# Attention's softmax sums on GpSimd: order of adds and joins, a third buffer of parts, later totals

## The reference

```python
c_q  = h_t @ W_DQ + b_DQ;   c_kv = h_t @ W_DKV + b_DKV        # 32 wide
q = concat(c_q @ W_UQ + b_UQ, c_q @ W_QR + b_QR)              # 8 heads of 128 + 32
k = concat(c_kv @ W_UK + b_UK, h_t @ W_KR + b_KR)
v = c_kv @ W_UV + b_UV
attn = softmax(q @ k.T / sqrt(160), axis=-1)
x = x + (attn @ v) @ W_O + b_O
```

## Time and profile before

| | |
|---|---|
| median of 3 runs | 766.88 us (766.19 to 766.91) |
| profiled execution | 765.69 us |
| its span, first to last instruction | 763.5 us |
| mean granted clock of TensorE | 0.984 |
| busy: PE, DVE, ACT, POOL | 94%, 76%, 60%, 72% |
| attention's loop of blocks | about 38 to 519 us of the span |

### The profile page before, as it was taken

The page is one execution under the profiler, slowest core; times in us unless marked ns, Lnnn a source line. Parts: engine busy times, 40 slices in busy tenths (PEclk is TensorE's granted clock), DMA queues, the critical chain, the costliest instruction groups (busy, mean ns, idle before and its releaser), DMA issues.

```text
span 763.5 us, 12866 instructions
## 1 busy us (share of the span) xinstructions
PE 718.2 (94%) x4432; PEld 480.1 (63%) x4432; DVE 583.6 (76%) x1211; ACT 461.3 (60%) x1069; POOL 550.8 (72%) x451
## 2 busy tenths in 40 slices
PE   7979999989989999989999998859989999999997
PEld 6655555655656566555566555427656679788885
DVE  7878788877877888878888887454788835868885
ACT  4257667756665776755775665634667860455553
POOL 6447888878778888878888887941679872346674
PEclk9999999999999999999999999979999999999999
DMA  6213647547546646645645745714000000022430
GB/s 151 80 36 60 127 86 137 112 84 138 112 84 117 132 84 125 126 84 107 136 91 111 139 85 111 139 28 115 1 0 2 1 1 1 1 65 80 134 111 28
DMA packets 41672, 64.17 MB, mean 84 GB/s; under 512 B 16380, under 2 KB 25613, under 8 KB 37640
## 3 DMA queue, kind: packets, MB, share of 16 engines
q0 software_dynamic: 12896, 48.76, 32.6%
q1 hardware_dynamic: 27432, 14.48, 7.2%
q10 hardware_dynamic: 1280, 0.12, 0.1%
HBM read 13.35 MB, written 1.10 MB: 19 GB/s over the span
## 4 chain that ended last, share of the span: by engine, by line
POOL 32%; DMA 28%; PE 24%; issue 8%; DVE 6%; ACT 1%; POOLq 0%; ACTq 0%; DVEq 0%
DMA part<-prob 27%; POOL part L929 10%; POOL w_v L951 8%; POOL hid_lo L1028 4%; POOL w_v L955 4%; PE ps L1898 4%; PE ps L1538 2%; POOL nrm L1008 2%; PE ps L1494 2%; PE ps L1938 2%; DVE mx L1082 2%; PE ps L1940 2%; PE ps L1939 2%; PE ps L1480 1%; POOL hid L1008 1%
## 5 line engine op out<-in xcount | busy, mean ns | idle before, releaser
L1082 DVE TENSOR_REDUCE mx<-ps 128x1 f32<-128x512 f32 x492 | 303.6, 681 | 77.2 <-PE ps L1480 77.1
L643 ACT ACTIVATE prob<-ps 128x512 f32<-128x512 f32 x512 | 263.2, 615 | 123.2 <-PE ps L1494 105.2
L1494 PE MATMUL ps<-q_cols,key 128*128 128x512 f32 x512 | 213.1, 420 | 12.8 <-ACT prob L643 12.8
L1480 PE MATMUL ps<-key,q_rows 128*128 128x512 f32 x512 | 206.3, 408 | 2.1 <-DVE key L1068 1.6
L929 POOL TENSOR_TENSOR part<-prob 128x512 f32<-128x512 f32 x128 | 184.1, 1496 | 1.5 <-ACT prob L643 1.0
L1494 PEld LDWEIGHTS ps<-q_cols,key 128*128 128x128 f32 x512 | 96.9, 190 | 80.0 <-issue 34.1
L1538 PE MATMUL ps<-prob,val 128*32 128x512 f32 x1024 | 124.6, 604 | 0.0
L1480 PEld LDWEIGHTS ps<-key,q_rows 128*128 128x128 f32 x512 | 97.0, 190 | 29.3 <-DVE mx L1082 9.9
L951 POOL TENSOR_TENSOR w_v<-part,pair 128x1024 f32<-128x1024 f32 x31 | 74.1, 2391 | 50.4 <-DMA part<-prob 50.4
L943 POOL TENSOR_TENSOR pair<-prob 128x512 f32<-128x512 f32 x62 | 87.7, 1567 | 5.1 <-ACT prob L643 5.1
L1028 POOL TENSOR_TENSOR hid_lo<-hid,hid_hi 128x512 fp32r<-128x512 f32 x44 | 61.5, 1407 | 38.7 <-ACT hid_hi L809 38.6
(11 more groups left out here) (284 smaller groups left out, 1129.7 us busy)
## 6 DMA issues: line engine op xcount, KB each, us to landing
part<-prob POOLq DMA_DIRECT2D x31, 1024.0 KB, 7.4
w_v<-part POOLq DMA_DIRECT2D x31, 512.0 KB, 4.9
g_all<-g_rows SPq DMA_DIRECT2D x9, 256.0 KB, 3.2
den<-den_sb SPq DMA_DIRECT2D x124, 0.5 KB, 1.8
g_all<-g_rows SPq DMA_DIRECT2D x6, 224.0 KB, 3.0
X<-in_L_attn_h_t_dram SPq DMA_DIRECT2D x4, 256.0 KB, 4.0
out_dram<-X SPq DMA_DIRECT2D x4, 256.0 KB, 2.6
g_all<-g_rows SPq DMA_DIRECT2D x6, 128.0 KB, 3.0
```

The source lines that it names most:

```text
L643: act.activation(prob[:, g % RING, :], ps[:, g % 3, :], ACT.Exp, scale=SCALE).then_inc(s_exp, 1)
L1082: dve.tensor_reduce(mx[:, n % 2, c % TPB, at:at + 1], ps[:, BANK["rows", 2 * lin + j], :], AX.X, ALU.max).then_inc(s_mrd, 1)
L1480: pe.matmul(ps[:, BANK["rows", 2 * lin + j], :], q_rows[:, k, i * P:(i + 1) * P], key[:, h % KBUF, c0:c0 + BLK], start=True, stop=True).th ...
L1494: pe.matmul(ps[:, g % 3, :], key[:, n // NB % KBUF, t * P:(t + 1) * P], q_cols[:, n % NB, :], start=True, stop=True).then_inc(s_sc, 1)
```

## The change

- GpSimd's list in block n becomes: parts 0, 1, 2, 3, `add_pairs(n-1)`, `late_sums(n)`, pair 0, pair 1, `join_parts(n-1)`. `add_pairs` writes in place into the parts, and the join goes from parts 1, 3 into parts 0, 2.
- `part` becomes a list of three buffers; the third lies in `w_v`, where `fin` was.
- totals(n-2) moves from slot 1 to the end of slot 6; its copy by ScalarE goes to tile 14; output moves from slot 6 (n-2) to slot 1 (n-3), and VectorE's denominators and accumulate from slot 6 to slot 2. Their items in the rotation of banks move along.
- `row_pairs` and `key_parts`: block 0 makes one chunk per slot and one key; the two further chunks and the key are made in blocks 1 and 2.
- Blocks 28 and 29 are not joined: TensorE sums four parts. In block 30 VectorE adds tiles 8-11 and 12-15 to the parts, and GpSimd only makes the parts.

```diff
--- before.py
+++ after.py
@@ -195,20 +195,22 @@
 
         def row_pairs(n, slot):
 
-            first = CPB * n + slot + LEAD + (min(slot // 2, AHEAD) if n == 0 else AHEAD)
-            count = 2 if n == 0 and slot in range(1, 2 * AHEAD, 2) else 1
+            first = CPB * n + slot + LEAD + min(max(n - 1, 0), AHEAD) + (1 if 1 <= n <= AHEAD and slot > 2 else 0)
+            count = 2 if 1 <= n <= AHEAD and slot == 2 else 1
             return [lin for lin in range(first, first + count) if lin < NCHUNK]
 
         def key_parts(n, slot):
 
-            if n == 0 and slot in (0, 4):
-                return [NB + slot // 4]
+            if n == 2 and slot == 4:
+                return [n + KLEAD]
+            if n <= 2:
+                return [n + NB] if slot == 0 else []
             return [n + KLEAD] if slot == 0 and n + KLEAD < H * NB else []
         U = 7
         A_BANK = (4, 2)
         KB_AT = H * C1
         prob = sb("prob", [P, RING, BLK])
-        part = sb("part", [P, 2, NG, BLK])
+        part_sb = sb("part", [P, 2, NG, BLK])
         pair = sb("pair", [P, 2, BLK])
         den_sb = sb("den_sb", [P, BLK])
         den = sb("den", [P, 2, TPB])
@@ -225,11 +227,11 @@
 
         def begun(n):
 
-            return 4 if n == 0 else 5 * n + 4
+            return 4 if n == 0 else 5 * n + 3
 
         def paired(n):
 
-            return 5 * n + 7
+            return 5 * n + 9
         s_join = sem("s_join")
         s_usb, s_ops, s_rden, s_acc = sem("s_usb"), sem("s_ops"), sem("s_rden"), sem("s_acc")
         s_ones, s_densb, s_dend = sem("s_ones"), sem("s_densb"), sem("s_dend")
@@ -238,7 +240,7 @@
 
 
 
-        SUMS_AT, OUT_AT = 1, 6
+        JOINED = NBLK - 4
 
         BANK, BEFORE, holds = {}, {}, {}
 
@@ -258,9 +260,13 @@
                     todo.append(("queries", n + 2))
                 if slot == 5 and n == 0:
                     todo += [("folded", 0), ("folded", 1)]
-                if slot == SUMS_AT and 2 <= n < NBLK - 1:
+                if slot == 1 and 3 <= n < NBLK - 1:
+                    todo.append(("out", n - 3))
+                if slot == 1 and n == NBLK - 2:
                     todo.append(("sums", n - 2))
-                if slot == OUT_AT and 2 <= n < NBLK - 1:
+                if slot == 6 and 2 <= n < NBLK - 2:
+                    todo.append(("sums", n - 2))
+                if slot == 6 and n == NBLK - 2:
                     todo.append(("out", n - 2))
             for item in todo:
                 place_item(item, 3 + turn % 4)
@@ -389,7 +395,7 @@
         AT_TW = D + E
         s_sc1, s_d1, s_e1, s_gt_ps, s_gt, s_gtl, s_z0 = (sem(n) for n in ("s_sc1", "s_d1", "s_e1", "s_gt_ps", "s_gt", "s_gtl", "s_z0"))
 
-        fin = w_v[:, :, :].rearrange("p (x h) d -> p x (h d)", x=TPB)[:, 0:2, :]
+        part = [part_sb[:, 0], part_sb[:, 1], w_v[:, :, :].rearrange("p (x h) d -> p x (h d)", x=NG)]
         with nc.sbuf_tensor("pT", [P, HP, S], F32) as pT:
             pass
         act_g = sb("act_g", [P, 2, BLK])
@@ -505,9 +511,12 @@
                     with nc.allow_non_contiguous_dma("128 x 4 words into one row"):
                         sp.dma_start(q_cols[SH:SH + 1, k, :].bitcast(F32).rearrange("a (p i) -> a p i", i=TPB),
                                      nmx[:, n % 2, :].bitcast(F32)).then_inc(s_shift, 16)
-                    if n >= 2:
+                    if 3 <= n < NBLK - 1:
+                        denominators(n - 3)
+                    if n == NBLK - 2:
                         denominators(n - 2)
 
+                denominators(NBLK - 3)
                 denominators(NBLK - 2)
 
 
@@ -637,7 +646,10 @@
                         act.wait_ge(s_sum, begun(n - 1))
                     elif g >= RING and t == 2 * NG:
                         act.wait_ge(s_pv, NW * n)
-                        act.wait_ge(s_late, 16 * n)
+                        if n < NBLK - 1:
+                            act.wait_ge(s_late, 16 * n)
+                        else:
+                            act.wait_ge(s_pair, 2 * n - 1)
                     elif g >= RING and t == 3 * NG:
                         act.wait_ge(s_pair, 2 * n)
                     act.activation(prob[:, g % RING, :], ps[:, g % 3, :], ACT.Exp, scale=SCALE).then_inc(s_exp, 1)
@@ -671,7 +683,7 @@
                     for t in range(NT):
                         if t == 4 and n >= 1:
                             sums(n - 1)
-                        if t == 2 * SUMS_AT + 2 and n >= 2:
+                        if t == (14 if n < NBLK - 2 else 4) and n >= 2:
                             sums_out(n - 2)
                         if t == 10 and n == NBLK - 1:
                             sums_out(n - 1)
@@ -923,16 +935,16 @@
 
                 def begin_sum(n, g):
 
-                    if n >= 2 and g == 0:
-                        pool.wait_ge(s_join, 16 * (n - 1))
+                    if n >= 3 and g == 0:
+                        pool.wait_ge(s_ones, n - 2)
                     ready(n, 2 * g + 1)
-                    pool.tensor_tensor(part[:, n % 2, g, :], tiles(n, 2 * g, 1)[:, 0, :], tiles(n, 2 * g + 1, 1)[:, 0, :], ALU.add).then_inc(s_sum, 1)
+                    pool.tensor_tensor(part[n % 3][:, g, :], tiles(n, 2 * g, 1)[:, 0, :], tiles(n, 2 * g + 1, 1)[:, 0, :], ALU.add).then_inc(s_sum, 1)
 
                 def late_sums(n):
 
                     ready(n, 3 * NG - 1)
                     pool.wait_ge(s_sum, begun(n))
-                    pool.dma_start(part[:, n % 2, :, :], tiles(n, 2 * NG, NG), accum_op=ALU.add).then_inc(s_late, 16)
+                    pool.dma_start(part[n % 3], tiles(n, 2 * NG, NG), accum_op=ALU.add).then_inc(s_late, 16)
 
                 def add_pair(n, j):
 
@@ -946,29 +958,32 @@
 
                     pool.wait_ge(s_late, 16 * (n + 1))
                     pool.wait_ge(s_pair, 2 * (n + 1))
+                    p = part[n % 3][:, bass.ds(0, 2, step=2), :]
+                    pool.tensor_tensor(p, p, pair[:, :, :], ALU.add).then_inc(s_sum, 1)
+
+                def join_parts(n):
+
+                    pool.wait_ge(s_sum, paired(n))
                     if n >= 1:
-                        pool.wait_ge(s_ones, n)
-                    pool.tensor_tensor(fin, part[:, n % 2, bass.ds(0, 2, step=2), :], pair[:, :, :], ALU.add).then_inc(s_sum, 1)
-
-                def join_parts(n):
-                    pool.wait_ge(s_sum, paired(n))
-                    pool.dma_start(fin, part[:, n % 2, bass.ds(1, 2, step=2), :], accum_op=ALU.add).then_inc(s_join, 16)
+                        pool.wait_ge(s_join, 16 * n)
+                    pool.dma_start(part[n % 3][:, bass.ds(0, 2, step=2), :], part[n % 3][:, bass.ds(1, 2, step=2), :],
+                                   accum_op=ALU.add).then_inc(s_join, 16)
 
                 for n in range(NBLK):
                     begin_sum(n, 0)
                     if n < 2:
                         columns(n + 2)
                     begin_sum(n, 1)
-                    if n >= 1:
+                    begin_sum(n, 2)
+                    begin_sum(n, 3)
+                    if 1 <= n < NBLK - 1:
                         add_pairs(n - 1)
-                    begin_sum(n, 2)
-                    if n >= 1:
-                        join_parts(n - 1)
-                    begin_sum(n, 3)
-                    if n < NBLK - 1:
+                    if n < NBLK - 2:
                         late_sums(n)
                         add_pair(n, 0)
                         add_pair(n, 1)
+                    if 1 <= n <= JOINED:
+                        join_parts(n - 1)
                     if n == NBLK - 2:
                         ln0_pool(pool, 0)
                 pool.memset(anchors2[:, :], 0.0).then_inc(s_aside, 1)
@@ -1088,6 +1103,16 @@
                     if n >= 2:
                         dve.wait_ge(s_shift, 16 * (n - 1))
                     dve.tensor_reduce(nmx[:, n % 2, :], mx[:, n % 2, :, :], AX.X, ALU.max, negate=True).then_inc(s_sel, 1)
+
+                def late_sums(n, j):
+
+                    at = (NT * n + NG * (2 + j)) % RING
+                    if j == 0:
+                        dve.wait_ge(s_sum, begun(n))
+                    else:
+                        dve.wait_ge(s_pair, 2 * n + j)
+                    dve.wait_ge(s_exp, NT * n + NG * (3 + j))
+                    dve.tensor_tensor(part[n % 3], part[n % 3], prob[:, at:at + NG, :], ALU.add).then_inc(s_pair, 1)
 
                 def key_biases(m, bank):
                     heads = slice(4 * m, 4 * (m + 1))
@@ -1175,13 +1200,18 @@
                             chunk_max(lin)
                         if slot == 2 and n == 0:
                             values()
-                        if slot == 5 - AHEAD and n < NBLK - 1:
+                        if CPB * (n + 2) - 1 in lins:
                             minus_max(n + 1)
-                        if slot == OUT_AT and 2 <= n < NBLK - 1:
+                        if slot == 2 and 3 <= n < NBLK - 1:
+                            denominators(n - 3)
```

(35 more changed lines are left out.)

1 line of the change is left out of this document (removed).

## The result

The changed kernel takes 786.95 us (786.48 to 787.2, 4 runs) beside 766.54 for the kernel before in the same set; the ratio is 1.0271 [1.0252, 1.0289]. The forecast of 772.7 had the sign right and under a third of the size: +5.8 against +20.4. The profiled run took 787.2, its span 785.5. Against 763.5 before, the landmarks of ScalarE's timeline say where the 22.0 are.

The account below looks back on a forecast made before the run. It took TensorE to set the steady blocks, with the late DMA costing 11.95 in all. Terms +15.1, +1.3, -7.3 and -3.3 sum to +5.8, so 766.88 + 5.8 = 772.7, range 768 to 777.

Parts of the forecast that it names:

- The pause and the bank order: Slot 3 of each steady block: TensorE's second row matmul waits for VectorE's accumulate, 1.78 lost, net +1.05 per block.
- The step that failed: Totals' den transfers, from slot 7 to slot 2: 7 us available where 3.8 are needed, so no wait.
- +15.1: The 24 blocks with keys: 15.03 each, 360.7 in all instead of 345.62.
- +1.3: The three blocks without keys: 14.55 each, 43.65 in all instead of 42.35.
- The old long blocks: Four of 27 blocks lasting 15.4 to 17.4, tile 8's exponential waiting for the late DMA; said to disappear.
- The join: Last on GpSimd's queue each block; said to have more than a block until its totals in slot 6.
- The end: Last blocks: TensorE's 9.61 wait and half clock go, -12.4, against +5.1 of new work; net -7.3 (-9 to -4).
- the bound of 4.7: VectorE's late sums in block 30: 4.7 each instead of 2.2 would add 2.5; the forecast took 0.
- The start: Blocks 0 to 2: block 0 about 5.1 shorter, blocks 1 and 2 take back 1.8; net -3.3 (-5 to 0).
- The clock rival: Steady blocks: the new pause drops TensorE's granted clock in 11 of 28 blocks, 16 more, 788.7; chance 0.22.
- the stated whole: Whole program: 766 to 790, leaving out the two faster cases and the worst of the clock.
- The pause does not form: Slot 3: VectorE reads the out bank before TensorE wants it, 27 x 1.78 = 48 less, 725; chance 0.10.

Follow-up runs that it names:

- Run 4: Changed kernel with the late DMA of tiles 8 to 11 adding only 64 of 512 columns (an eighth of its bytes); 778.49 us.
- run 6: Changed kernel with totals of n-2 in slot 1 of every block; 860.4 us with accumulation in slot 1, 909.08 us with it in slot 2.
- run 9: Block 30's tiles 8 to 15 given back to GpSimd, without VectorE's late sums: 787.94 us on the changed kernel, 748.45 with accumulation in slot 1, totals in slot 4.
- run 1: Changed kernel with only the totals two slots earlier, in slot 4; accumulation stays in slot 2; 787.21 us.
- Run 5: Changed kernel with the late DMA cut to an eighth of its bytes and accumulation in slot 1; totals stay in slot 6; 735.84 us.
- Run 3: Changed kernel with both accumulation in slot 1 and totals in slot 4; 744.75 us.
- run 2: Changed kernel with only VectorE's denominators and accumulation moved from slot 2 to slot 1; 783.33 us.

## Why the prediction was wrong in size

In the profiled executions +5.8 became +22.0. Of the 16.2 between them 8.7 are the five long blocks, 3.1 the even blocks, 2.2 the end, 0.3 the start, and 1.7 the clock's fall in the FFN, which has nothing to do with the change.

- **The pause and the bank order held.** Place, releaser and number (28) are as worked out. It is 1.53 of idle; from start to start it costs 1.70, and 0.10 more at the start behind it: 1.80, where 1.78 was worked out. The even block is 15.15 against 15.03, and 14.60 against 14.55, as the bank waits that went away were some 0.63 and not 0.73: 24 x 0.12 = 2.9 too little, and 0.15 in the other three.
- **The step that failed** is "Totals and the den transfers that SP issues start at slot 7 and have 7 us until slot 2, where 3.8 are needed." The 3.8 were read where these transfers lay beside the end of the late DMA alone. The change moves them towards its start, and the join by DMA behind them. Each lands in 4.0 at the median and 5.0 at most, the four take 3.7 to 5.7 to issue, and the last lands 5.5 to 8.6 behind the first issue: there were 7.8 until the reciprocal (7.3 without keys), a little more than the 7, and five times that was not enough. The step was put at nothing in the sum. In the 24 blocks four long ones hold 2.29 + 2.27 + 0.71 + 0.51 = 5.8, which with the 2.9 makes 8.7 of the 8.8 between +15.1 and +23.9. The fifth holds 2.9 of the 3.1 between +1.3 and +4.4. Run 4 takes the large transfer away and gets 8.5 back. The old long blocks, where ScalarE waited for the late DMA, did disappear as forecast; new ones of another cause came. I had counted what each queue issues, and not what is in flight when it does.
- **The join** was said to have "more than a block until its totals in slot 6". It is issued at the start of the block in whose slot 6 its totals stand, so it had about 12 us of the 15. That did no harm here, and was paid in run 6.
- **The end** gave 5.1 instead of 7.3. The 9.61 is gone, and the late sums took 2273 ns each, the 2.2 that I took and not the bound of 4.7. But I had looked only at whether GpSimd slows them, not at what they do to GpSimd and to the norm behind:

```profile
519.03 2.26 DVE L1115 TENSOR_TENSOR part<-part,prob 128x2048 f32<-128x2048 f32 x1
519.21 2.18 POOL L339 TENSOR_SCALAR vare<-mv 128x4 f32<-128x4 f32 x1 [4.10 <-DVE mv L333]
522.50 4.96 POOL L941 TENSOR_TENSOR part<-prob 128x512 f32<-128x512 f32 x4
522.55 5.14 DVE L359 TENSOR_SCALAR hn<-X,mv,rstd 128x128 f32<-128x128 f32 x4 [1.26 <-POOL rstd L341]
```

GpSimd's vare takes 2.18 beside the second late sum, as it ends with it, and 0.24 in run 9's kernel without the sums. Four hn of 0.34 take 5.14 beside four part adds of 4.96. TensorE then waits 2.00 for hn at 527.84. And behind block 30's own pause, 2.00 by the bank order as worked out, the granted clock was 0.50 from 509.3 to 512.8, which the sum did not have. What each of these takes of the 2.2 is not told apart.
- **The start** gave 3.0 for 3.3.
- **The clock rival** (788.7) named a time near the measured one, by another way, and the stated whole reached to 790 on its account; that the measured time lies in it is luck. The pause of 1.53 came in 22 blocks and the clock stayed at 1.00 behind it; in runs 1 and 4, where 27 blocks in a row have it and none of these a longer one, none is long. It fell behind four pauses of 2.00 to 2.90. Three of these were longer for what was late, and the fourth is block 30's, which runs 1 and 4 have too. So in the loop the clock is a consequence of the late transfers, but it is more than half of what they cost: 4.7 of 8.7.
- **"The pause does not form"** had 725 for a kernel without it. Run 5 (735.84) shows why that was too low: the small bank waits come back when the pause goes. Run 3 (744.75) has no pause either, but pays for the totals' place and for the join.

## What to carry to other kernels

A transfer's time belongs to its moment: before moving a small transfer, look at what large one is in flight where it will be issued, and price it there. When a wait is taken away, the next candidate stands right behind it, and here each of two edits was worth next to nothing alone and 42 us together; so test a pair before dropping its halves. And before placing a consumer earlier, follow its producer to the slot in which it is issued, with the block index written out: three slots too many cost 116 in run 6 (860.4 against 744.75).

## What the runs showed of the chip

- The transfers of 128 words each that SyncE issues for the totals land in 1.8 us (median) where only the end of GpSimd's accumulating transfer of 1 MB lies beside them, and in 4.0 where most of it does, with one of 512 KB behind it; each issue takes 1050 ns instead of 584. With an eighth of the bytes, in more and smaller packets, it is 1.7 and 584 (run 4). Which resource the two share these runs do not tell.
- The granted clock stayed at 1.00 through 27 pauses of 1.53 to 1.58 in a row, one a block of 15 (runs 1 and 4). In the changed kernel it fell to 0.50 after pauses of 2.26, 2.23, 2.90 and 2.00, and after others of 2.23 and 2.02 it did not; in run 2's trace it stayed at 1.00 after 2.77, 2.63 and 2.43; and in the kernel before it was 0.50 from 45.8 to 49.2, where the longest wait just ahead is the 1.57 of the earlier trace rows. So the length alone does not decide it. A fall in the loop cost 1.57.
- Beside VectorE's add of two SBUF inputs, GpSimd stood until that add was done even for an operation on 4 elements a partition (2.18 against 0.24), and four operations of VectorE that read SBUF (0.34 each otherwise) took as long as GpSimd's adds beside them (5.14 and 4.96). The Trainium skill (SBUF — State Buffer, Who interferes with whom) states this as an exclusive lock, and these rows agree.
